# One instruction of 1024 columns for two neighbouring mask tiles on VectorE, in a masked attention block on one core

## The reference

```
h = jnp.maximum(_layernorm(x, axis=-1), 0.0)
q, k, v = heads(h @ Wq + bq), heads(h @ Wk + bk), heads(h @ Wv + bv)
scores = jnp.einsum('bhqd,bhkd->bhqk', q, k) * scale
scores = jnp.where(mask[:, None] == 0, -jnp.inf, scores)
attn = jax.nn.softmax(scores, axis=-1)
out = jnp.einsum('bhqk,bhkd->bhqd', attn, v)
x = x + (out.transpose(0, 2, 1, 3).reshape(b, s, D_MODEL) @ Wo + bo)
```

## Time and profile before

| | |
|---|---|
| median of three runs | 1573.6 us (1569.19 to 1575.42) |
| profiled execution, its own time | 1572.28 us |
| its span, first to last instruction | 1570.4 us |
| mean granted TensorE clock | 0.998 of full speed |
| busy PE / DVE / ACT / POOL | 1543.7 / 1445.6 / 1413.3 / 756.6 us |
| masks on VectorE (718 and 721) | 512 + 74 instructions, 367.0 + 66.1 us |
| masks on GpSimd (453) | 438 instructions, 577.2 us |

### The profile page before, as it was taken

How to read it: one execution, slowest core, us unless ns; L and a number is a source line. 1 busy time by engine, 2 the same in 40 slices (tenths; PEclk the granted TensorE clock), 3 DMA queues, 4 the chain that set the end, 5 groups by cost and what they waited for, 6 DMA issues and landing times.

```text
span 1570.4 us, 27696 instructions
## 1 busy us (share of the span) xinstructions
PE 1543.7 (98%) x7580; PEld 1049.7 (67%) x7580; DVE 1445.6 (92%) x3505; ACT 1413.3 (90%) x3433; POOL 756.6 (48%) x674
## 2 busy tenths in 40 slices
PE   7999999999999999999999999999999999999998
PEld 5666666666666666666666666666666766666754
DVE  7899999999999999999999999999999999999887
ACT  3899899999989999999999989989999999999985
POOL 3245445445454544545544553544644544553453
PEclk9999999999999999999999999999999999999999
DMA  7544443534444344443444444444443544434330
GB/s 226 122 113 110 129 112 99 145 96 132 108 122 128 95 139 102 137 111 100 142 102 132 110 117 133 98 136 102 131 121 90 150 104 127 115 101 118 95 99 28
DMA packets 154065, 183.65 MB, mean 117 GB/s; under 512 B 67748, under 2 KB 69808, under 8 KB 153904
## 3 DMA queue, kind: packets, MB, share of 16 engines
q1 hardware_dynamic: 149024, 179.76, 42.1%
q10 hardware_dynamic: 4888, 2.11, 0.6%
HBM read 54.79 MB, written 16.78 MB: 46 GB/s over the span
## 4 chain that ended last, share of the span: by engine, by line
PE 64%; DVE 15%; ACT 11%; issue 6%; SPq 2%; ACTq 1%; DMA 1%; DVEq 0%
PE psP L874 29%; PE psO L998 11%; PE ps L965 11%; PE ps L977 10%; DVE ps L704 6%; ACT ps L548 5%; ACT probs L606 4%; DVE probs L718 3%; DVE neg_max L704 1%; DVE oT_lo L738 1%; ACT hT_hi L520 1%; ACTq L502 1%; DVE stats L629 1%; SPq L292 1%; DVE x_tile L637 1%
## 5 line engine op out<-in xcount | busy, mean ns | idle before, releaser
L453 POOL TENSOR_TENSOR probs<-probs,keep_k 128x512 int32<-128x512 int32 x438 | 577.2, 1341 | 532.9 <-ACT probs L606 532.1
L704 DVE CUSTOM_DVE_ANT_0 ps<-ps,bias_q 128x512 f32<-128x512 f32 x1024 | 703.5, 693 | 85.9 <-PE ps L965 79.9
L548 ACT ACTIVATE ps<-ps,neg_max 128x512 f32<-128x512 f32 x1024 | 691.3, 675 | 77.7 <-DVE neg_max L704 63.9
L606 ACT ACTIVATE probs<-ps 128x512 f32<-128x512 f32 x1024 | 622.4, 609 | 38.5 <-PE psO L998 20.0
L965 PE MATMUL ps<-k_stack,q_stack 96*128 96x512 f32 x1024 | 424.3, 415 | 8.4 <-ACT ps L548 4.9
L977 PE MATMUL ps<-q_stack,k_stack 98*128 98x512 f32 x1024 | 416.1, 407 | 2.8 <-ACT probs L606 1.6
L718 DVE SCALAR_TENSOR_TENSOR probs<-turned,probs 128x512 f32<-128x512 bf16 x512 | 367.0, 718 | 5.1 <-ACT probs L606 4.3
L965 PEld LDWEIGHTS ps<-k_stack,q_stack 96*128 96x128 f32 x1024 | 193.1, 189 | 115.7 <-ACT ps L548 42.4
L998 PE MATMUL psO<-probs,v_sb 128*32 128x512 f32 x2048 | 246.5, 598 | 1.0 <-issue 1.0
L977 PEld LDWEIGHTS ps<-q_stack,k_stack 98*128 98x128 f32 x1024 | 194.4, 190 | 70.7 <-ACT probs L606 38.1
L548 ACT ACTIVATION_READ_ACCUMULATOR ps<-ps,neg_max 128x1 f32 x1024 | 222.9, 218 | 0.0
(11 more groups left out here) (97 smaller groups left out, 1951.7 us busy)
## 6 DMA issues: line engine op xcount, KB each, us to landing
k_stack<-oT_hi SPq DMA_DIRECT2D x380, 64.0 KB, 2.0
q_stack<-y_tile SPq DMA_DIRECT2D x360, 64.0 KB, 2.0
x_tile<-in_x_dram SPq DMA_DIRECT2D x66, 256.0 KB, 3.0
y_tile<-in_x_dram SPq DMA_DIRECT2D x62, 256.0 KB, 2.9
out_dram<-y_tile SPq DMA_DIRECT2D x62, 256.0 KB, 2.1
turned<-in_adj_dram SPq DMA_DIRECT2D x61, 256.0 KB, 2.9
q_stack<-part_hi SPq DMA_DIRECT2D x240, 64.0 KB, 2.0
k_stack<-oT_lo SPq DMA_DIRECT2D x196, 64.0 KB, 2.0
```

The lines of the kernel that those rows point to most:

```text
L453: nc.gpsimd.tensor_tensor(bits, bits, keep_k[:, kt // 2, :], ALU.mult).then_inc(gpsimd_masked, 1)
L548: nc.scalar.activation(item, item, ACT.Exp, scale=-1.0, bias=neg_max[:, g % 2, col:col + 1], accum_out=exp_sum[:, col:col + 1]).then_inc(e ...
L606: nc.scalar.activation(probs[:, (SLOTS * b + n) % P_RING, :], ps2[:, n % 2, :], ACT.Exp, scale=SCALE).then_inc(exp2_done, 1)
L704: nc.vector.tensor_tensor_reduce(bank1(k, ("s", u)), bank1(k, ("s", u)), bias_q[:, qt, :], -SCALE, 3.0e38, ALU.add, ALU.min, neg_max[:, g ...
```

## The change

Where the two tiles of an even and the following odd number are both VectorE's, the mask of the even one is left out in its slot, and in the slot of the odd one both are masked by one instruction of 1024 columns. The mask operand is the same 512 columns read twice (a broadcast), and the output is two neighbouring tiles of the ring. The semaphore `vector_masked` rises by two. Before, a group of 16 tiles had nine masks on VectorE; now it has four double ones and one single one. Over the kernel that makes 260 double masks and 66 single ones in place of 586.

```diff
-                    if have(b) and not on_gpsimd(b, n):
+                    if have(b) and not on_gpsimd(b, n) and not (n % 2 == 0 and not on_gpsimd(b, n + 1)):
 
                         kt = n % 16 // 4
+                        first = n - 1 if n % 2 and not on_gpsimd(b, n - 1) else n
+                        heads = n + 1 - first
...
                         dve.wait_ge(exp2_done, due(64 * b + n + 1))
-                        tile = probs[:, (SLOTS * b + n) % P_RING, :]
+                        at = (SLOTS * b + first) % P_RING
+                        tile = probs[:, at:at + heads, :]
                         if kt % 2 == 0:
-                            nc.vector.scalar_tensor_tensor(out=tile, in0=bias_k[:, kt // 2, :], scalar=-MASKED, in1=tile,
-                                                           op0=ALU.add, op1=ALU.min).then_inc(vector_masked, 1)
+                            bias = bias_k[:, kt // 2:kt // 2 + 1, :].to_broadcast([P, heads, S])
+                            nc.vector.scalar_tensor_tensor(out=tile, in0=bias, scalar=-MASKED, in1=tile,
+                                                           op0=ALU.add, op1=ALU.min).then_inc(vector_masked, heads)
```

More of the change, by code:

```diff
@@ L715, in step @@
                         dve.wait_ge(exp2_done, due(64 * b + n + 1))
-                        tile = probs[:, (SLOTS * b + n) % P_RING, :]
+                        at = (SLOTS * b + first) % P_RING
+                        tile = probs[:, at:at + heads, :]
                         if kt % 2 == 0:
-                            nc.vector.scalar_tensor_tensor(out=tile, in0=bias_k[:, kt // 2, :], scalar=-MASKED, in1=tile,
-                                                           op0=ALU.add, op1=ALU.min).then_inc(vector_masked, 1)
-                        else:
-                            nc.vector.scalar_tensor_tensor(out=tile, in0=keep_k[:, kt // 2, :], scalar=-MASKED, in1=tile,
-                                                           op0=ALU.mult, op1=ALU.min).then_inc(vector_masked, 1)
+                            bias = bias_k[:, kt // 2:kt // 2 + 1, :].to_broadcast([P, heads, S])
+                            nc.vector.scalar_tensor_tensor(out=tile, in0=bias, scalar=-MASKED, in1=tile,
+                                                           op0=ALU.add, op1=ALU.min).then_inc(vector_masked, heads)
+                        else:
+                            keep = keep_k[:, kt // 2:kt // 2 + 1, :].to_broadcast([P, heads, S])
+                            nc.vector.scalar_tensor_tensor(out=tile, in0=keep, scalar=-MASKED, in1=tile,
+                                                           op0=ALU.mult, op1=ALU.min).then_inc(vector_masked, heads)
                     if u in C_AT:
```

## The result

The changed kernel takes 1599.9 us (median of four runs, 1599.5 to 1600.2) against 1572.6 before: ratio 1.0173, 95% interval 1.0161 to 1.0185. It is 27 us slower. The prediction had 1578 and a range up to 1588, so even its slow rival was too small.

What follows compares the result with a forecast made beforehand. TensorE was taken to set the pace for most of a step. 15 steps x (0.59 lost - 0.32 gained) = +4.1 us, plus 0.5 at the end, gave 1576.9, put at 1578 us; range 1566 to 1588.

Steps and rivals of the forecast that it cites:

- slow rival: Double masks hold the port shared with GpSimd, making T(21) or T(37) late: 0.45 us a step, 1585 us; chance 0.28.
- case (b): Slots 32 and 24, VectorE ahead of TensorE: T 0.53 us late, losing 0.45 and 0.14, 0.59 us a step.
- the paragraph behind it: GpSimd's masks of tiles 4 and 12 may wait up to 0.5 us at slots 16, 24, 32, under about 1 us slack.
- What a mask costs: A double mask lasts about 1.22 us and holds VectorE 1.14 us, so a pair saves 0.08 us.
- One sign: Over the whole kernel, VectorE busy for some 45 us less, by lengths of the masks.
- Case (a): VectorE behind, slots 5 to 12 and 44 to 54: two pairs ahead gain 0.16 us each, 0.32 us a step.
- the sign that the prediction named: Slots 5 to 12: the way from T(5) to the scores of slot 11 shorter by 0.16 us.
- Case (c): Slots 16, 30 and 40, where T waits for its scores: delay hidden by ScalarE's slack, costing nothing.
- The end: Last step, slot 48 on: a double mask ends 0.53 us later and TensorE waits, +0.5 us once.
- The sum: Whole kernel: 15 full steps x (0.59 - 0.32) = +4.1 us, and +0.5 at the end: +4.6 us.
- The two ends of what a pair could save: Bounds on how long a double mask holds VectorE: 1.05 us (saving 0.17) or 1.22 us (nothing saved).

Runs made afterwards that it cites:

- x2: The kernel before with only the pair of slot 24 (tiles 26 and 27) as a double mask: 1591.2 us, ratio 1.0135.
- x3: The changed kernel, but GpSimd's mask of tile 12 in slot 24 also waits until line 647 of that slot is done: 1582.2 us, ratio 1.0070.
- x7: The changed kernel with line 647 of slot 24 moved to slot 23, ahead of the double mask: 1578.1 us, ratio 1.0043.
- x8: The kernel before, all masks single, but line 647 of slot 24 waits until GpSimd's mask of tile 12 is done: 1589.7 us, ratio 1.0109.
- x1: The changed kernel with the pair of slot 24 (tiles 26 and 27) masked by two single instructions again: 1576.6 us, ratio 1.0041.
- x10: The kernel before with the mask of tile 34 moved from slot 31 to slot 32 as a single instruction: 1579.8 us, ratio 1.0060.
- x4: The kernel before with only the pair of slot 32 as a double mask: 1578.9 us, ratio 1.0052.
- x11: The kernel before with double masks only in the nine pairs where VectorE is behind, and none in the last batch: 1569.4 us, ratio 0.9992.
- x5: The kernel before with double masks only in the nine pairs where VectorE is behind, in all batches: 1567.7 us, ratio 0.9978.
- x6: The changed kernel with the pairs of slots 24 and 32 as single masks: 1569.8 us, ratio 0.9988.
- x9: The kernel before with the mask of tile 26 moved from slot 23 to slot 24, both masks still single instructions: 1594.7 us, ratio 1.0151.

## Why the prediction was wrong

**The step that failed** is in case (b) and in the paragraph behind it. "The same happens once more at slot 24 ... 0.39 of the 0.53 are absorbed, 0.14 us are left" took the double mask as 0.53 us more of VectorE and nothing else. "GpSimd's masks of tiles 4 and 12 may wait for a double mask at slots 16, 24 and 32, up to 0.5 us, under the slack of about 1 us" saw that GpSimd is made to wait, and asked only whether GpSimd can afford it. It never asked who stands behind the double mask on VectorE and needs the port next. At slot 24 that is line 647. It lost its turn to the waiting GpSimd and stood still for 1.10 us, most of a GpSimd mask. In place of 0.14 us the slots lost 1.36 (changed kernel) and 1.35 (x2); with the order put back 0.26 (x3) or 0.01 (x7); and with the order alone 1.26 (x8). That is shown, and it is 21 to 23 of the 27 us (x1).

The margin was in the trace of before, 0.10 us between 673.80 and 673.90, and was not looked for. The slow rival named the right resource and the right direction of the first wait, but its place was T(21) and T(37) behind the single int32 mask, and its price 0.45 us. Neither happened as written: the int32 masks of 512 columns did not get longer in the mean (864 ns after, 898 before).

```profile
L721 DVE SCALAR_TENSOR_TENSOR probs<-keep_k,probs 128x512 f32<-128x512 int32 x74 | 66.1, 898 | 3.0 <-ACT probs L606 2.8
```

```profile
L726 DVE SCALAR_TENSOR_TENSOR probs<-keep_k,probs 128x512 f32<-128x512 int32 x66 | 57.0, 864 | 0.9 <-ACT probs L606 0.7
L726 DVE SCALAR_TENSOR_TENSOR probs<-keep_k,probs 128x1024 f32<-128x1024 int32 x4 | 6.7, 1663 | 3.2 <-ACT probs L606 3.2
```

**What a mask costs** was right. Double masks are 1.22 us long (median 1220 ns), and where VectorE is behind, the next T starts 1.13 us later, at 657.52 and 658.65. x10 against x4 gives 0.07 us for the pair. One sign failed. VectorE was to be busy for some 45 us less by lengths; its masks took 39 us less (433.1 and 393.8), but its busy time rose by 11.3 us (1445.6 and 1456.9). Line 647 alone added 16.5 (25.6 and 42.1). The page counts an overlap of two instructions once, so what a pair saves by lengths is not what it saves in busy time.

**Case (b) at slot 32** was right in place, mechanism and size. 0.45 was predicted, 0.49 measured in the changed kernel and 0.52 in x4. S2(38) starts 0.47 us after S(38) (702.01 and 701.54), where it was 0.23 us before (691.25 and 691.02):

```profile
696.66 0.69 DVE L704 CUSTOM_DVE_ANT_0 ps<-ps,bias_q 128x512 f32<-128x512 f32 x1
...
701.35 0.60 ACT L606 ACTIVATE probs<-ps 128x512 f32<-128x512 f32 x1
...
701.54 0.39 PE L970 MATMUL ps<-k_stack,q_stack 96*128 96x512 f32 x1
...
702.01 0.50 PE L982 MATMUL ps<-q_stack,k_stack 98*128 98x512 f32 x1
```

E2(36) at 701.35, S2(38) at 702.01: 0.66 us, the closest distance that the prediction had read from the earlier trace rows.

**Case (a)** was half right. Slots 50 to 4 gained 0.12 of 0.16 us: 0.11 to 0.13 in each of the eight kernels with double masks there, and 0.03 at most in the others. In slots 5 to 12 the sign that the prediction named came true and the gain did not. From T(5) to the scores of slot 11 it is 7.84 us in place of 8.05, shorter by some 0.2 where 0.16 was forecast. But T(5) comes 0.1 us later against its scores than before (2.00 and 1.89), and the -0.07 of the table is no more than x2 has with single masks there.

The delay of T(5) is the same exchange of turns at a second place. In slot 4 the int32 mask, GpSimd's line 436 and VectorE's line 653 (16 columns, for the softmax constants) meet. If line 436 starts first, the int32 mask waits for it (1.67 us) and line 653 is short (0.16). If the int32 mask is first, line 436 gets in behind it, and line 653 waits. The second case, from the changed kernel, one step after the one used so far:

```profile
746.85 0.94 DVE L726 SCALAR_TENSOR_TENSOR probs<-keep_k,probs 128x512 f32<-128x512 int32 x1
747.71 1.27 DVE L653 TENSOR_TENSOR c_all<-neg_max,c_all 128x16 f32<-128x16 f32 x1
...
747.20 1.75 POOL L436 TENSOR_TENSOR y_tile<-y_tile,bo_row 128x512 f32<-128x512 f32 x1
```

Then T(5) is about 0.35 us later. Of the 12 steps, the kernels with single masks in slots 62 to 8 have this in one to three (before: 3), those with double ones in five to nine (changed: 5). Why the doubles make it more frequent was not tested. x11 has nine such steps and x5 five, its slots 5 to 12 take 0.15 us longer in a step, and over 15 steps that covers the 1.7 us between them.

T(8), moved ahead by a mask, gains nothing either, since it meets ScalarE's queue (ACTq) in the middle of issuing two transfers:

```profile
656.90 0.70 DVE L704 CUSTOM_DVE_ANT_0 ps<-ps,bias_q 128x512 f32<-128x512 f32 x1
657.52 1.22 DVE L722 SCALAR_TENSOR_TENSOR probs<-turned,probs 128x1024 f32<-128x1024 bf16 x1
658.65 0.69 DVE L704 CUSTOM_DVE_ANT_0 ps<-ps,bias_q 128x512 f32<-128x512 f32 x1
...
657.14 1.17 ACTq L502 DMA_DIRECT2D q_stack<-c_rows  x2
658.36 0.66 ACT L548 ACTIVATE ps<-ps,neg_max 128x512 f32<-128x512 f32 x1 [0.63 <-issue]
```

T(8) is done at about 657.6, and E1(8) starts at 658.36. As a whole the case exists: x5 is 0.2% faster. It is at the edge of what can be told, since x11, the same kernel up to the last batch, is within 0.1% of the kernel before.

**Case (c)** at slots 16, 30 and 40 was not quite nothing: slots 22 and 23 lost 0.13 us in the changed kernel, and 0.05 to 0.08 with less around it (x1, x6). The pairs of slots 14 and 38 stand in none of the three cases, so the delay may be that of slot 14 or of slot 16; no run parts the two. Slots 31 to 35 and 39 to 49 showed no loss.

**The end** was mis-sized: 0.5 predicted, 1.4 by the traces.

**The sum** with the measured sizes is 15 x 1.73 = 26.0 and 1.4 at the end, 27.4 us, against 27.3 by the medians (27.2 by the spans of the two profiles). The two ends of what a pair could save (1.05 and 1.22 us) played no part. One exchange of turns, not bounded at all, was five times the whole net estimate.

## What to carry to other kernels

When an instruction is made longer or moved on an engine that shares a port, list who will be waiting when it ends, on both sides, and what the loser's wait holds up; the price is up to the other engine's whole instruction (here 1.10 us of a mask of 1.29), not the time by which something moved. A margin of a tenth of a microsecond between the starts of two such instructions is a term of the sum with two values, and both belong in the range. Where merged work takes the place of work that filled a hole, charge the delay at the next engine whose distance to its consumer is already at its minimum; that rule gave 0.45 where 0.49 was measured, and 0.14 where 0.26 was left once the order was put back (x3).

## What the runs showed of the hardware

- Line 647 of VectorE (one input, int32 to bf16, input and output in SBUF, 0.42 us alone) waits until a GpSimd instruction that got in first is done: 1.52 us. Line 653 (two inputs of 16 columns in SBUF, 0.16 us alone) does so too: 1.27 us. Line 738, with an input in PSUM, runs at 0.74 us beside GpSimd. But line 629, whose one input and output lie in SBUF, is not held up either: 0.69 us at 676.02 of the kernel before, in the middle of the three GpSimd masks shown above (673.90 to 677.90). So "everything in SBUF" is not by itself what makes an instruction wait, and no run here shows what does.

```profile
676.02 0.69 DVE L629 BATCH_NORM_STATS2 stats<-x_tile 128x6 f32<-128x512 f32 x1
```

- The wait shows as length of the waiting instruction (1.52 us), not as idle time of its engine; only with a semaphore does it show as a wait (1.44 us, x8). Neither the table of waits nor the idle column points to it; the maximum in the view of the line does.
- Two masks of 512 columns in a row hold VectorE for 1.21 us (684.41 to 685.62), one of 1024 for 1.14 us. In x9 GpSimd became ready 0.10 us after the second of the two had started (685.12 and 685.02) and in x10 0.26 us after it, and came in behind it both times. Whether it would get in between two masks if it were waiting earlier, no run shows.
